# One load of four input blocks in place of three loads

## What is computed

```python
Wc = conv_w[:, :, 0, 4]
def step(prev, x_i):
    y = jnp.einsum('oc,nch->noh', Wc, prev) + conv_b[None, :, None]
    y = jnp.where(y >= 0, y, prelu_a * y)
    cur = y + x_i
    return (cur, cur)
_, fwd_rest = jax.lax.scan(step, x[0], x[1:])
_, bwd_rest = jax.lax.scan(step, fl[-1], fl[:-1], reverse=True)
# group norm of v, per n and group of 16 channels
m = jnp.mean(g, axis=(2, 3, 4)); s = jnp.var(g, axis=(2, 3, 4))
g = (g - m) / jnp.sqrt(s + eps)
x = x + conv_scan(group_norm(x))
```

## Time and profile before

| | |
|---|---|
| Median of 3 runs | 376.71 us |
| The profiled execution, its time | 376.45 us |
| Its span, first to last instruction | 374.7 us |
| Lies around the span | 1.75 us |
| PE busy | 351.7 us (94%) |
| DVE busy | 286.4 us (76%) |
| ACT busy | 230.1 us (61%) |
| POOL busy | 17.3 us (5%) |
| Chain that ended last, by engine | PE 91%, DMA 6% |

### The profile page before, as it was taken

One profiled execution on the slowest core, in us unless ns is written; L12 is line 12 of the kernel. 1 busy time (PEld: TensorE's weight loads), 2 busy tenths in 40 slices (PEclk: granted clock), 3 DMA queues, 4 the chain that ended last, 5 costly groups with the idle time before them and its releaser, 6 DMA issues.

```text
span 374.7 us, 10100 instructions
## 1 busy us (share of the span) xinstructions
PE 351.7 (94%) x3100; PEld 350.4 (93%) x3100; DVE 286.4 (76%) x925; ACT 230.1 (61%) x810; POOL 17.3 (5%) x30
## 2 busy tenths in 40 slices
PE   0279999999999999999999999999999999999996
PEld 0169999999999999999999999999999999999996
DVE  2688899788887887665666878778778787787786
ACT  4776656656556566565565665656656657566564
POOL 2078000000000000000000000000000000000000
PEclk9999999999999999999999999999999999999999
DMA  8998000000000000000000121212212212122122
GB/s 308 433 406 310 2 0 1 0 0 0 1 0 0 1 0 0 0 0 0 0 0 0 59 83 57 84 64 76 84 56 84 79 61 84 60 80 84 56 112 84
DMA packets 10232, 26.30 MB, mean 70 GB/s; under 512 B 1264, under 2 KB 1520, under 8 KB 9712
## 3 DMA queue, kind: packets, MB, share of 16 engines
q1 hardware_dynamic: 10224, 26.22, 18.1%
HBM read 13.63 MB, written 12.58 MB: 70 GB/s over the span
## 4 chain that ended last, share of the span: by engine, by line
PE 91%; DMA 6%; SPq 1%; DVE 1%; ACT 1%; issue 0%; ACTq 0%
PE psum L352 88%; DMA xin<-in_x 6%; SPq L234 1%; PE psum L312 1%; PE psum L302 1%; DVE state L535 0%; DVE state L530 0%; ACT state L382 0%; ACT state L376 0%; PE psum L277 0%; PE psum L273 0%; PE psum L266 0%; ACT above L445 0%; PE psum L295 0%; PE psum L289 0%
## 5 line engine op out<-in xcount | busy, mean ns | idle before, releaser
L352 PE MATMUL psum<-state,w_t 128*128 (+1 forms) x2976 | 332.6, 275 | 0.0
L352 PEld LDWEIGHTS psum<-state,w_t 128*128 128x128 f32 x2976 | 332.5, 192 | 0.0
L445 ACT ACTIVATE above<-psum,params 128x128 f32<-128x128 f32 x376 | 139.9, 372 | 129.4 <-PE psum L352 128.6
L530 DVE TENSOR_TENSOR state<-above,state 128x128 f32 (+1 forms) x376 | 108.4, 288 | 65.9 <-ACT above L445 64.9
L447 ACT ACTIVATE below<-psum,negative 128x128 f32<-128x128 f32 x376 | 140.1, 373 | 0.0
L535 DVE SCALAR_TENSOR_TENSOR state<-below,negative,state 128x128 f32 (+1 forms) x376 | 123.5, 349 | 6.8
L582 DVE TENSOR_TENSOR state<-state,xin (+1 forms) x45 | 30.8, 684 | 0.0
L457 DVE BATCH_NORM_STATS2 bstat<-xin 128x6 f32<-128x512 f32 x32 | 20.3, 677 | 11.2 <-DMA xin<-in_x 11.2
L475 DVE TENSOR_SCALAR state<-xin,mean,rstd 128x320 f32<-128x320 f32 (+2 forms) x72 | 28.0, 435 | 0.0
L266 PE MATMUL psum<-chan,centre 128*128 128x64 f32 (+1 forms) x8 | 2.1, 360 | 17.1 <-DVE chan L471 17.1
L266 PEld LDWEIGHTS psum<-chan,centre 128*128 128x128 f32 x8 | 1.6, 250 | 17.4 <-issue 13.9
(11 more groups left out here) (38 smaller groups left out, 27.7 us busy)
## 6 DMA issues: line engine op xcount, KB each, us to landing
out_y<-state SPq DMA_DIRECT2D x47, 256.0 KB, 2.0
xin<-in_x SPq DMA_DIRECT2D x4, 1536.0 KB, 13.9
xin<-in_x SPq DMA_DIRECT2D x5, 768.0 KB, 19.9
xin<-in_x SPq DMA_DIRECT2D x7, 256.0 KB, 18.6
w_t<-in_w SPq DMA_DIRECT2D x4, 256.0 KB, 9.9
xin<-in_x SPq DMA_DIRECT2D x1, 512.0 KB, 23.6
out_y<-state SPq DMA_DIRECT2D x1, 192.0 KB, 1.9
out_y<-state SPq DMA_DIRECT2D x1, 64.0 KB, 1.6
```

The source lines that it names most:

```text
L352: mm = nc.tensor.matmul(psum[:, 4 * par + o, 0:COLS], w_t[:, k, o * P:(o + 1) * P], xs[k], start=k == 0, stop=k == 3)
L445: nc.scalar.activation(above[:, par, o, :], z, ACT.Relu, bias=params[:, o:o + 1], scale=1.0).then_inc(above_done, 1)
L530: nc.vector.tensor_tensor(sts[o], above[:, par, o, :], sts[o], ALU.add).then_inc(part_done, 1)
```

## The change

`PAIRS`, a table from the first block of a pair to the second, becomes `TOGETHER`, a table from the first block of a transfer to the number of blocks in it. It has the same pairs from block 4 on, and blocks 0 to 3 are one transfer. All blocks of a transfer share its semaphore, so the waits on blocks 0 to 3 are now one and the same wait. The order of the instructions on DVE, ACT, PE and POOL is the same.

```diff
-PAIRS = {2: 3, 4: 5, 6: 7, 8: 9}
+TOGETHER = {0: 4, 4: 2, 6: 2, 8: 2}
...
-        for first, second in PAIRS.items():
-            x_loaded[second] = x_loaded[first]
+        for first, count in TOGETHER.items():
+            for b in range(first + 1, first + count):
+                x_loaded[b] = x_loaded[first]
...
-            for b in (b for b in range(NBLK) if b not in PAIRS.values()):
-                n1 = (PAIRS[b] if b in PAIRS else b) % N + 1
+            for b in (b for b in range(NBLK) if b == 0 or x_loaded[b] is not x_loaded[b - 1]):
+                n1 = b % N + TOGETHER.get(b, 1)
```

## The result

The changed kernel takes 380.0 us, the median of 6 runs (379.64 to 380.16), where the kernel before, run beside it, takes 376.63 us (376.55 to 376.83, 6 runs). The ratio is 1.0087, with a 95% interval of 1.0076 to 1.0097: slower by 3.4 us. The profiled execution has 380.09 us and a span of 378.1 us, against 374.7 before.

The account below looks back on a forecast made before the run. The prediction took a PE-bound scan of fixed length, starting when the statistics are done: ACT's 4.12 us delay less 0.25 and 0.15 us gives 3.7, added to 376.71 for 380.4 us, range 378.9 to 382.6.

Parts of the forecast that it names:

- Landings: Input stream: blocks 0 to 3 land together at 10.9 us, everything behind as before; bounds 0.3 us earlier, 0.5 us later.
- ACT's sum: ACT's queue from 11.00 us through block 6: ends at 24.87 us instead of 20.75, 4.12 us later.
- DVE close to ACT but in front: DVE reaches `channel_stats(6)` at about 24.5 us, before ACT's 24.87, so ACT sets this point.
- PE from k = 1 on: PE's queue: group values of k = 1 move from 21.20 to 25.32 us, last sums come 3.7 us later.
- the change of pace moves along with the work: PE's switch from 232 to 121 ns per matmul shifts with its work; otherwise the shift is 2.5 or 7.3 us.
- 0.25 + 0.15 back: PE regains 0.25 us from block 12's landing wait and 0.15 from a wait for ACT, off the 4.12 us.
- The near tie: Before the scan: POOL free for block 15's `rstd` at about 39.5 us, wanted at 39.65; if late, so is the end.
- The sum: Whole kernel: 376.71 us plus a 3.7 us later scan start gives 380.4 us.
- Caught up: Rival: later waits absorb the backlog and the stream's end still sets the time, 376.7 us; chance 0.05.
- faster: Rival: the stream gains a fixed cost for each load removed, 376.4 us or 375.2; chance 0.03.
- The case of DVE and ACT as the bound: Rival: PE's fast pace comes early, so DVE and ACT bind; shift 2.0 to 2.9 us, 379.1 us; chance 0.14.
- 4 us for two loads: Input stream: by the skill's page, two transfers fewer would save an estimated 4 us; not used in the sum.

Follow-up runs that it names:

- the early table load: A 1-element activation ahead of ScalarE's first wait for data: 378.6 us in the changed kernel, 376.67 us in the kernel before.
- two and two: Kernel before, with blocks 0 and 1 in one load and 2 and 3 in one (16 loads): 376.38 us, ratio 0.9991.
- four single loads: Blocks 0 to 3 in four loads, 18 in all, instead of the changed kernel's one joint load: 376.72 us, ratio 1.0001.
- the repeat: The changed kernel run once more, unaltered, in another set: 380.13 us, ratio 1.0093.
- the wait alone: Kernel before with its 17 loads, but VectorE and ScalarE wait for the load of blocks 2 and 3 before they begin: 379.83 us, ratio 1.0086.
- three and one: Blocks 0 to 2 in one load and block 3 alone (16 loads), instead of the changed kernel's joint load: 377.99 us, ratio 1.0034.
- the three with more work on PE: Changed kernel with extra idle matmuls in PE's early pause: 24 instructions 379.33 us, 12 instructions 379.98 us, 12 plus an early table load 378.13 us.
- less work on POOL: Changed kernel with POOL's second group of columns of k = 1 normalised by VectorE during the first scan steps: 380.26 us, ratio 1.0093.

## Why the prediction was right, point by point

- **Landings.** Right. The joint load should be used at 10.9 to 11.0 us, and was at 10.99 to 11.02. The old loads with the new wait gave the time of the new load within 0.3 us. (The prediction's "3.69 and 3.68" for a pair are 3.67 and 3.69 by the rows, and two single blocks at 1.75 are 3.50, so a pair was if anything the dearer.)
- **ACT's sum.** Right, to the hundredth: block 6 was to end at 24.87 us and did. Such a sum is this good because ACT runs the same instructions in the same order, and each length comes from a row. The table load in it was right too: 1.3 us when it is taken out, and nothing in the kernel before.
- **DVE close to ACT but in front.** Right: it waited for ACT at four joins up to `channel_stats(6)` (24.96 us, as predicted).
- **PE from k = 1 on.** The start at 25.32 and the variances at 28.9 came as predicted. The step that failed is "I take it that the change of pace moves along with the work", together with the wait of 0.25 us before block 12 that was taken as all that PE had to spare. The rows, first of the kernel before, then of the changed kernel:

```profile
25.23 2.27 PE L302 MATMUL psum<-same_group 128*128 128x128 f32 x12
...
28.71 0.33 PE L266 MATMUL psum<-chan,centre 128*128 128x64 f32 x2
```

```profile
31.53 0.33 PE L267 MATMUL psum<-chan,centre 128*128 128x64 f32 x2
```

  From the variances of k = 1 to the group values of k = 2 PE took 31.53 - 28.90 = 2.63 us instead of the 28.71 - 24.79 = 3.92 less a wait of 0.25; so 1.0 us more came back. Half of it went into a wait for ACT at the variances of k = 2 (0.63 us, where 0.07 had been left). The term "0.25 + 0.15 back" measured 4.12 - 3.17 = 0.95 us at the last sums. The trace that the 0.25 came from was not typical. The same two groups of idle instructions in the kernel before with the early table load (376.67 us, the same work on PE):

```profile
25.15 1.56 PE L303 MATMUL psum<-same_group 128*128 128x128 f32 x12
...
27.87 1.13 PE L303 MATMUL psum<-same_group 128*128 128x128 f32 x8 [1.17 <-DMA xin<-in_x]
```

  The twelve took 1.56 us and not 2.27, and the wait for block 12 was 1.17 us and not 0.25; in the kernels with two and two and with four single loads it was 0.99 us. So a wait read from one execution was too small by some 0.8 us, because PE's pace happened to rise late in it. The time didn't show it, since the landing of block 12 came last either way.
- **POOL.** The near tie was real and was decided against the kernel. POOL was free near 39.3 us (predicted 39.5), but PE's sums came sooner than predicted, so POOL's last power (ending at 39.82) was the last to arrive. The loss can be read along POOL alone. Its power of k = 1 began 29.79 - 25.97 = 3.82 us later, and the 0.46 us for which it had waited before block 15 were given back, which leaves 3.36 us; the scan began 3.32 us later. From the start of that power to the scan's second step it took 42.22 - 29.79 = 12.43 us in the changed kernel and 12.42 to 12.44 in seven other traces (the repeat, the wait alone, three and one, the early table load, and the three with more work on PE), while the twenty idle instructions took from 2.45 to 3.45 us in them. So from the variances of k = 1 on it is POOL's queue that sets the scan's start in these kernels, and PE's pace behind them shows only when it is later still, as with less work on POOL (PE's queue was some 0.24 us behind). The prediction had both queues and put PE's first; that its 3.7 lies close to the 3.4 measured owes something to the two being so near each other.
- **The sum.** 3.7 us predicted for the start of the scan, 3.32 in the trace, 3.4 in the times. The late start, ACT's backlog and the fixed scan behind them were right. The term for what PE gives back was too small by 0.55 us, and POOL, the last to arrive, took 0.15 of that again.
- **The rivals.** "Caught up" was rightly small for four blocks and is what happens for two; "faster" through a price for each load is refuted by four single loads. The case of DVE and ACT as the bound (2.0 to 2.9 us) didn't come, though PE did wait 0.63 us for ACT on the way.

The Trainium skill, "DMA: Bandwidth & Descriptors", section "Anatomy of one DMA", has about 2.0 us for each DMA on GpSimd's path, and says that most of it is the time until completion is confirmed. The prediction's 4 us for two loads read it as time of the stream. Here, on SyncE's queue with loads standing behind each other, a load more moved the last landing by 0.2 us, and two loads fewer left it within 0.1 us.

Open is what sets the moment at which PE's pace changes. The same twenty instructions behind the variances of k = 1 took 2.47, 2.77 and 3.67 us in three traces with the same PE work ahead of them (the changed kernel, its repeat, and the one with less POOL work).

## What to carry to other kernels

The joint load saved nothing here, where the loads stood behind each other in the queue anyway, and it delayed all the work that waits for its first part. The cost was not the delay but what was left of it after the waits of the busiest consumer: a start 1.7 us later cost nothing, 3.6 us cost 1.3 and 5.5 us cost 3.4. Add up that engine's queue from the new landing, with everything queued behind its first wait (a table load among it), and see whether it waits for data again before the stream ends; in these kernels the loss was gone where it did. Then follow each queue behind it, POOL's as well as PE's, to the first step. And take the slack of an engine whose pace varies from more than one execution: the 0.25 us read from one trace were about 1 us in three others.

## What the hardware showed unexpectedly

PE's pace (232 ns for a matmul instruction, then 121 ns) changed at another moment in each execution, at the same work. The twenty idle instructions behind the variances of k = 1 took from 2.45 to 3.67 us in six traces of kernels that do the same on PE from the group values of k = 1 on. Where the stream sets the end, twelve took 1.56 us in three traces and 2.27 in the kernel before. So one pair of traces can't tell whether the pace moves with the work: by these lengths, in the changed kernel the fast pace came some 2 us later than in the trace of the kernel before, but some 4 us later, like the work, than in the three others. More work ahead of it gave no clear picture either: twelve instructions more didn't bring it forward (20 in 3.22 us), 24 more did (the next twelve in 1.50 us), and twelve fewer put it back (20 in 4.42 us). The granted clock doesn't show the change: it reads 1.00, the level of 2.4 GHz, from 20 to 24 us as well as from 31 to 34 us, in the kernel before and in the changed one. Only the lengths of the matmuls do. The times of the kernels with more idle matmuls spread from 379.05 to 380.28 us, against 376.55 to 376.83 for the kernel before; that this spread comes from the pace ahead of the variances is likely but not shown.
